# A fused attention and mixture-of-experts kernel: the base layer three tiles behind the attention instead of two, the power fold on GpSimd ahead of the fifth gather, the last two rolls added one slot later

## The reference

```python
# 1: a LoRA adapter of the sample, rank 16
Bx = einsum('bni,bri->bnr', x, B[adapter_ids]); y = einsum('bnr,bor->bno', Bx, A[adapter_ids])
# 2: auto-correlation attention along the 1024 values
f = rfft(y); corr = irfft(f * conj(f)); weights, delay = top_k(corr, 6)
x = x + sum_k softmax(weights)[k] * y[(i + delay[k]) % 1024]
# 3: the channels of a sample are mixed with one of 16 64x64 matrices
z = einsum('bct,bcd->bdt', x, W[condition])
# 4: base layer, bias, and the two best of 8 LoRA experts of rank 16 (router: softmax, top 2)
x = x + z @ W_base.T + b_base + lora(z, combine)
```

## Time and profile before

| | |
|---|---|
| median of 3 runs | 948.55 us (945.19 to 948.85) |
| the profiled execution, its own time | 951.79 us |
| its span, first to last instruction | 950.0 us |
| mean granted TensorE clock | 0.94 of full speed |
| TensorE, VectorE, GpSimd, ScalarE busy | 804.7, 622.3, 482.7, 336.9 us |
| matmuls of the base layer (line 464, `o_ps`) | 512 x3, 430, 395 and 395 ns each |
| `add_rolled`, line 942 | 160 of 1431 ns |
| `bias_added`, line 1085 | 32 of 2408 ns |

### The profile page before, as it was taken

One profiled execution on the slowest core, in us unless ns is written; L12 is line 12 of the kernel. 1 busy time (PEld: TensorE's weight loads), 2 busy tenths in 40 slices (PEclk: granted clock), 3 DMA queues, 4 the chain that ended last, 5 costly groups with the idle time before them and its releaser, 6 DMA issues. The chain is left out here.

```text
span 950.0 us, 16005 instructions
## 1 busy us (share of the span) xinstructions
PE 804.7 (85%) x4808; PEld 668.9 (70%) x4808; DVE 622.3 (66%) x1362; ACT 336.9 (35%) x617; POOL 482.7 (51%) x465
## 2 busy tenths in 40 slices
PE   4555899998888988888988988888888889889887
PEld 3545787777776776677766877777676777678776
DVE  2245767867676676767667686767567677677772
ACT  5343334333333333333443334334333334233311
POOL 1244555735475553755556464745427555455530
PEclk9755999999999999999999999989979999999998
DMA  8476587666666766775757667665856758677541
GB/s 279 125 207 206 180 256 227 193 220 208 216 198 208 236 211 206 219 211 183 250 190 236 208 215 231 197 206 175 253 152 215 211 184 253 201 235 234 174 137 45
DMA packets 66940, 194.47 MB, mean 205 GB/s; under 512 B 13724, under 2 KB 24380, under 8 KB 63684
## 3 DMA queue, kind: packets, MB, share of 16 engines
q0 software_dynamic: 23040, 83.90, 28.5%
q1 hardware_dynamic: 32084, 71.33, 26.8%
q10 hardware_dynamic: 11760, 38.66, 10.4%
HBM read 118.35 MB, written 50.33 MB: 178 GB/s over the span
## 5 line engine op out<-in xcount | busy, mean ns | idle before, releaser
L1096 POOL DMA_INDIRECT rolled<-y_d,off x160 | 175.1, 1094 | 272.6 <-DVE row L942 159.0
L942 DVE SCALAR_TENSOR_TENSOR row<-rolled,weight,row 128x1024 f32<-128x1024 f32 x160 | 228.9, 1431 | 116.3 <-DMA rolled<-y_d,off 113.3
L464 PE MATMUL o_ps<-wt_hi,x_hi 128*128 128x512 f32 x512 | 220.4, 430 | 0.0
L464 PE MATMUL o_ps<-wt_hi,x_lo 128*128 128x512 f32 x512 | 202.4, 395 | 0.0
L464 PE MATMUL o_ps<-wt_lo,x_hi 128*128 128x512 f32 x512 | 202.3, 395 | 0.0
L572 PE MATMUL x_ps<-mix,row 128*128 128x128 f32 x512 | 80.9, 323 | 77.3 <-DVE row L942 56.2
L572 PEld LDWEIGHTS x_ps<-mix,row 128*128 128x128 f32 x512 | 74.0, 230 | 91.1 <-DVE row L942 48.2
L1085 POOL TENSOR_TENSOR row<-row,bias 128x1024 f32<-128x1024 f32 x32 | 77.1, 2408 | 111.7 <-PE x_ps L572 111.7
L464 PEld LDWEIGHTS o_ps<-wt_hi,x_lo 128*128 128x128 f32 x512 | 96.6, 189 | 22.6
L464 PEld LDWEIGHTS o_ps<-wt_hi,x_hi 128*128 128x128 f32 x512 | 97.1, 190 | 19.3 <-issue 4.8
L464 PEld LDWEIGHTS o_ps<-wt_lo,x_hi 128*128 128x128 f32 x512 | 97.6, 191 | 14.6
(11 more groups left out here) (130 smaller groups left out, 1471.7 us busy)
## 6 DMA issues: line engine op xcount, KB each, us to landing
y_d<-y ACTq DMA_DIRECT2D x64, 512.0 KB, 4.4
row<-in_x SPq DMA_DIRECT2D x32, 512.0 KB, 5.7
adapter<-g_hi SPq DMA_DIRECT2D x64, 256.0 KB
out<-row SPq DMA_DIRECT2D x32, 512.0 KB, 2.8
adapter<-g_lo SPq DMA_DIRECT2D x32, 256.0 KB
r<-in_L_cond_A SPq DMA_DIRECT2D x72, 64.0 KB
r<-in_L_cond_B SPq DMA_DIRECT2D x56, 64.0 KB, 2.0
rolled<-in_L_ffn_W_base SPq DMA_DIRECT2D x5, 512.0 KB, 5.7
```

The source lines that it names most:

```text
L464: last = pe.matmul(dst, a, b, start=start and n == 0, stop=stop and n == len(todo) - 1)
L942: dve.scalar_tensor_tensor(row[u][:, :], rolled[n % RB][:, :], weight[:, n:n + 1], row[u][:, :], ALU.mult, ALU.add).then_inc(sum_step, 1)
L1096: pool.indirect_dma_start(out=rolled[n % RB][:, :], out_offset=None, in_=y2_d[u], in_offset=bass.IndirectOffsetOnAxis(ap=off[:, n:n + 1], ...
```

## The change

Five things change together.

LAG becomes 3: tile t = s - 3 is in the base layer while tile s is in the attention, so there are 35 slots instead of 34. There are five row buffers instead of four, and three mixing matrices instead of four (their load now waits for the `mixed` that used the buffer, and stands behind the store in SyncE's queue).

Roll 3 and roll 4 of a tile are added one slot later, behind the delays of the next tile, and the gathers run through the three `rolled` buffers without a break between tiles. `mixed` takes tile s-2 (`m`) instead of s-1. The router is in two halves.

On GpSimd gathers 0 to 3 come first, then the bias, then `powers`, and gather 4 last.

`b_times_x` and `bx_repeated` write into `t_ps`, the banks of x transposed, instead of `c_ps`; the wait for the delays of the tile before moves from `b_times_x` to `correlation`. The copy of x transposed is first in ScalarE's slot, and both halves of the transposition stand together. `hc` has a buffer of its own, `h_transposed` stands at c = 5 and `ht_hi` behind the copy of y, `ft` lies in `r2`, and `off` is doubled.

The hardware loop is gone: all 35 slots are written out, and the registers that held the waits' values with it.

```diff
-LAG = 2
+LAG = 3
...
-        bx_ps = c_ps[:, P:2 * P]
-        s_ps = c_ps[0:STK, 0:P]
+        bx_ps = t_ps[:, 0:P]
+        s_ps = t_ps[0:STK, 512:512 + P]
...
-        def slots(eng, slot):
-            for s in range(U):
+        def slots(slot):
+            for s in range(NT + LAG):
                 slot(s, s % U, s // U)
-            with eng.Fori(1, NG - 1) as i:
-                for u in range(U):
-                    slot(i * U + u, u, i)
-            for s in range(NT - U, NT + LAG):
-                slot(s, s % U, s // U)
...
             def b_times_x(s, u, i):
-                if from_first(s):
-                    pe.wait_ge(top_step, TOPS * (s - 1) + 2)
...
             def correlation(s):
+                if s > 0:
+                    pe.wait_ge(top_step, TOPS * (s - 1) + 2)
...
-                if has(s - 1):
+                if has(m):
...
-                    mixed(s - 1, *before(u, i, 1))
+                    mixed(m)
...
                 if has(last):
-                    top_delays(last, ul % 2)
+                    top_delays(last, last % 2)
                 if has(t):
-                    router(t)
+                    router(t, 0)
+                if has(m):
+                    add_rolled(m, 3)
+                    add_rolled(m, 4)
+                if attn and s > 0:
+                    bx_masked(s)
                 if has(last):
                     weights(last)
-                    add_y(last, ul)
+                    add_y(last)
+                if attn and s > 0:
+                    stack_low(s)
...
+                if has(t):
+                    router(t, 1)
                 if has(last):
-                    add_rolled(last, ul, 0)
+                    add_rolled(last, 0)
+                    if u == 2 and has_group(g):
+                        spectrum_low(g)
+                    add_rolled(last, 1)
...
                 if has(last):
-                    for n in range(1, NSEL):
-                        if n == 2 and u == 2 and has_group(g):
-                            spectrum_low(g)
-                        add_rolled(last, ul, n)
+                    add_rolled(last, 2)
...
+            def gather(s, u, ns):
+                for n in ns:
+                    at = NSEL * s + n
+                    if n == 0:
+                        pool.wait_ge(top_step, TOPS * s + 5)
+                        pool.wait_ge(y_saved, 32 * (s + 1))
+                    if n == 3:
+                        pool.wait_ge(top_step, TOPS * s + 11)
+                    if at >= RB:
+                        added, of = (at - RB) // NSEL, (at - RB) % NSEL
+                        pool.wait_ge(sum_step, SUMS * added + of + 2)
...
             def slot(s, u, i):
                 t, last, g = s - LAG, s - 1, i + 1
+                if has(last):
+                    gather(last, (u - 1) % U, range(4))
                 if has(t):
-                    bias_added(t, (u - LAG) % U)
-                if has(last):
-                    gather(last, (u - 1) % U)
+                    bias_added(t)
                 if has_attn(s):
                     powers(s)
+                if has(last):
+                    gather(last, (u - 1) % U, range(4, NSEL))
```

More of the change, by code:

```diff
@@ L42 @@
 NCE = Q + 2
-LAG = 2
+LAG = 3
 U = 4
+NROW = 5
+NMIX = 3
 RB = 3
@@ L131, in build @@
         tiles(nc, locals())
-def wait_apart(eng, regs, holds, *waits):
-    if all(isinstance(value, int) for _, value in waits):
-        regs = []
-    else:
-        for reg, (_, value) in zip(regs, waits):
-            eng.reg_mov(reg, value)
-        eng.wait_ge(*holds)
-    for n, (sem, value) in enumerate(waits):
-        eng.wait_ge(sem, regs[n] if regs else value)
 def tiles(nc, v):
@@ L358, in w_at @@
             return t_ps if m in (0, 2, 3) else o_ps
-        def first(s):
-            return isinstance(s, int) and s == 0
         @blk.sync
         def _(sp):
-            regs = [sp.alloc_register(f"sp_wait{n}") for n in range(3)]
             x_t = x.rearrange("(t b) c l -> t (b c) l", b=SPT)
@@ L451, in _ @@
             load_a(1)
-            slots(sp, slot)
-            for u in range(U):
-                sp.wait_ge(out_saved[u], 16 * NT // U)
+            slots(slot)
+            for n in range(NROW):
+                sp.wait_ge(out_saved[n], 16 * len(range(n, NT, NROW)))
         @blk.tensor
@@ L646, in slot @@
                         adapter_out(s, u)
-                    if first(s) and c in (4, 5):
+                    if c == 5 and ffn:
+                        h_transposed(t)
+                    if s == 0 and c in (4, 5):
                         w_transposed(KC - 6 + c)
@@ L696, in _ @@
             pe.wait_ge(g_lo_sp, 1)
-            slots(pe, slot)
+            slots(slot)
         @blk.scalar
@@ L877, in _ @@
             w_high(5)
-            slots(act, slot)
+            slots(slot)
         @blk.vector
         def _(dve):
-            regs = [dve.alloc_register(f"dve_wait{n}") for n in range(2)]
             def low(dst, src, hi):
@@ L1024, in slot @@
                 if has(t):
-                    ut = (u - LAG) % U
+                    rows = row[t % NROW]
                     dve.wait_ge(out_mm, t + 1)
                     dve.wait_ge(biased, t + 1)
-                    dve.tensor_tensor(row[ut][:, :], o_ps[:, :], row[ut][:, :], ALU.add).then_inc(out_add, 1)
-                if has(last):
+                    dve.tensor_tensor(rows[:, :], o_ps[:, :], rows[:, :], ALU.add).then_inc(out_add, 1)
+                if has(m):
                     for h in range(2):
-                        dve.wait_ge(x2_h, 2 * last + 1 + h)
+                        dve.wait_ge(x2_h, 2 * m + 1 + h)
                         low(x2_lo[:, 4 * h:4 * h + 4, :].rearrange("p k r -> p (k r)"),
@@ L1049, in _ @@
             w_low(5)
-            slots(dve, slot)
+            slots(slot)
         @blk.gpsimd
         def _(pool):
-            regs = [pool.alloc_register(f"pool_wait{n}") for n in range(3)]
-            for u in range(U):
-                pool.memset(mix[u][:, :], 0.0)
+            for n in range(NMIX):
+                pool.memset(mix[n][:, :], 0.0)
             pool.memset(eo[:, 4, :], 0.0).then_inc(cleared, 1)
@@ L1140, in _ @@
             pool.wait_ge(bias_in, 16)
-            slots(pool, slot)
+            slots(slot)
 _INS = ["x", "itok_B_4_50", "itok_B_0_15", "L0_cond_A", "L0_cond_B", "L0_cond2_weights", "L0_ffn_W_base",
```

248 lines of the change are left out of this document (125 added, 123 removed).

## The result

The changed kernel takes 1003.64 us (median of 4 runs, 1001.5 to 1006.35) against 948.51 for the kernel before: ratio 1.0591, 95% interval 1.055 to 1.0633. It is slower, as forecast, but by 55 us where 30 were forecast, and it lies outside the range. The profiled execution took 1006.35 us, its span is 1004.6, its mean granted clock 0.91.

What follows compares the result with a forecast made beforehand. GpSimd's chain (gather 3, bias, powers, then `eo_hi`, `eo_lo`) was taken to set each slot. 951.8 + 25 (steady part) - 7.5 (head) + 12.7 (tail) = 982, as median 979, stated 978 us; range 944 to 996.

Steps and rivals of the forecast that it cites:

- the plain slot of 27.3: Slot 3, u = 3 and slots 28 to 31, 11 in all: 25.9 us each, 27.3 with the lowered clock.
- u = 1 was put at 30.0: Six slots where `mixed` waits for `fold_out` behind `eo_hi`: 28.4 us each, 30.0 with the lowered clock.
- forecast 1.4: After TensorE's wait of 4.3 us, correlation and `project` run at lowered clock: +1.4 us, at best nothing, at most 1.6.
- The bias as +2.4 in the chain: On GpSimd the bias, moved between gather 3 and the powers, adds 2.4 us to the chain ahead of `eo_lo`.
- the split as a gain: On GpSimd gather 4 moves out of the way of the powers: -1.4 us in the chain.
- each of the two blocks the other: Bias on GpSimd ran 2.41 us while a three-element VectorE step took 2.31 instead of 0.16, each blocking the other whole.
- `eo_lo` at 0.83 in every kind of slot: VectorE's last step before the correlation was counted at 0.83 us, after `eo_hi` at 0.74.
- 28.7 and 26.4: Slot lengths in us at u = 0 (with the lowered clock) and u = 2 (clock stays up), six slots each.
- the sum of 811: Slots 3 to 31 after the change, with the clock: 300 + 172 + 180 + 158 = 811 us, against 786.1 before.
- the clock holds (945): Rival, 12%: the chain lengthens as forecast but TensorE's clock does not fall, 945 us.
- the order of issue costs 0.9 more in 23 slots (1001): Rival, 10%: two rolls inside the powers instead of one, and the clock's fall on all the wait's neighbours, 1001 us.
- TensorE becomes the bound (906): Rival, 18%: rolls and GpSimd's steps hardly collide, powers end before about 20.5 in a plain slot, 906 us.

Runs made afterwards that it cites:

- e4: The changed kernel with unused 128-column matmuls in TensorE's waits (80 at u = 0, 60 at u = 1, 40 at u = 3 and without preparation): 997.9 us.
- e5: As e4 with fewer unused matmuls (56 at u = 0, 40 at u = 1, 22 at u = 3, 34 without preparation): 990.4 us.
- e6: The changed kernel with GpSimd's bias ahead of gather 0, where the kernel before has it: 973.3 us, ratio 1.031 to the kernel before.
- e9: e6 with the bias waiting for `eo_lo` of the tile before and the preparation for `eo_lo` of its own tile: 899.4 us, ratio 0.948.
- e10: The changed kernel with bias and powers behind all five gathers again: 1070.1 us, ratio 1.128 to the kernel before.
- e11: The changed kernel with B times x and its repeat back in the correlation's banks, the maxima wait back ahead of B times x: 1004.1 us.
- e1: The changed kernel with GpSimd's preparation at u = 0 and u = 2 waiting until `eo_lo` is finished: 970.6 us, ratio 1.020 to the kernel before.
- e2: The kernel before with its hardware loop written out, nothing else changed: 936.4 us, ratio 0.986.
- e3: e1 with bias and powers between gathers 2 and 3 on GpSimd: 865.8 us, ratio 0.912 to the kernel before.
- e7: e3 without the wait of the preparation for `eo_lo` that e1 added: 868.4 us, ratio 0.918 to the kernel before.

## Why the prediction was right or wrong

**Direction, chain, clock: right.** As forecast, the correlation waits for `eo_lo`, and no longer `mixed` for rolls; GpSimd's chain sets the slot; the plain slot of 27.3 is 27.2; u = 1 was put at 30.0 and is 29.3; the clock fell to 0.93, and e4 and e5 put its price at 1.5 to 1.9 a slot where it held (forecast 1.4). The bias as +2.4 in the chain is borne out by the clear plain slots of e6 and by e9, the split as a gain by e10 (a larger one than forecast), the banks as nothing by e11. One reading was too strong: the earlier trace rows shows VectorE's step held for the bias, but not that "each of the two blocks the other", for the bias took 2.41 there, its usual 2.408. For roll 2 against the powers the loss was 1.0, near the 0.9 that the forecast took from a row.

**The step that failed** is `eo_lo` at 0.83 in every kind of slot. The forecast itself wrote that the folds end the slot at u = 0 on GpSimd, and that they "cost the next one about 0.5", but never asked what VectorE does in their first microseconds. In the kernel before, the preparation started behind the powers directly and `eo_lo` came later, behind roll 4. Its view by tile there (ns, min/median/max) and GpSimd's low part of the adapters in slot 14:

```profile
L886 DVE TENSOR_TENSOR eo_lo<-eo,eo_hi x32: 809/820/2980, 57.3 to 903.0; 128x640 fp32r<-128x640 f32 x32
```

```profile
439.60 3.34 POOL L1080 TENSOR_TENSOR g_lo<-r,g_hi 128x1024 fp32r<-128x1024 f32 x1
```

It was done when `eo_lo` started, at 443.9; at u = 0 `eo_lo` took 1.11 there in five of the six slots, a part of one fold, and 1.89 in slot 4. The 2.98 is slot 18, and there the same meeting stands in the trace of before: the low part ran from 548.28 to 551.62, and the correlation waited 0.94 us for `eo_lo`.

```profile
549.32 2.98 DVE L886 TENSOR_TENSOR eo_lo<-eo,eo_hi 128x640 fp32r<-128x640 f32 x1
```

So the meeting, and what it does to `eo_lo`, could have been read in the trace of before. The change takes roll 4 from in front of `eo_lo` and puts gather 4 in front of the preparation, and the two meet in all twelve slots. The terms of the sum that came out too low are 28.7 and 26.4, measured 31.2 and 28.6; e1 takes the collision away and finds 28.8 and 26.1, and 970.6 in all, within the range. The rule about the shared reads was applied to roll 2 and the powers, where it cost what was forecast (1 us).

**A cause inside the 786.** The loop's back edges were named as not being in the sum; writing the loop out is worth 12 to 15 us (e2), near the 18 of VectorE's time that five waits of 3.6 make, though not in the slots where those waits stood. It is no part of the miss, since the sum of 811 was added up from chains without it.

**Rivals.** That the clock holds (945) and that the order of issue costs 0.9 more in 23 slots (1001) were both wrong as mechanisms; the second names nearly the right time for a wrong reason. It wanted two rolls inside the powers in 23 slots: the powers take 4.8 us, the length with one collision, in 21 of the 29 slots, and 5.7 to 5.8 only in the six at u = 2, where the forecast already had two. That TensorE becomes the bound (906) needed the powers to end before 20.5. In the changed kernel they end at 23.1; e3, with them at 19.5, shows that the condition was the right one, and that the gain beyond it is larger, 866.

**Where the gain of the later rolls went.** They freed `mixed`, and the freed time was used up in front of the correlation: roll 0 ends some 3 us later behind rolls 3 and 4 (9.9 to 12.9 in the forecast, 13.8 with the clock), the bias is 2.4, the collision 2.7 at u = 0 and u = 2. With bias and powers no longer behind a roll it comes back, 135 us (e7), which is 68 us less than the kernel before with its loop written out.

## What to carry to other kernels

When a wait is removed, list what stands in front of the next one and move that list first: here one gather more behind the powers in GpSimd's order (e7) turned a loss of 6% into a gain of 8%. For each instruction that is last in a chain and has two SBUF inputs on VectorE, look up what GpSimd starts in the same microsecond, in every kind of slot and not only in the plain one; it can be the next slot's work too, as with the bias in e6. An engine's order has to be tried together with the lag that feeds it: powers ahead of gather 3 took 135 us off with three tiles of lag and the later rolls, and added 171 with neither.
